# A recurrent layer on one core: its loop written out, its x blocks prefixed and transferred in halves, one product and three copies moved

## What is computed

```
x = x + attn0(rnn(x, cond))          # rnn: h = tanh(x_t @ Wx + h @ Wh + b), step by step, h kept for all t
x = x + ffn0(gru(x, cond))
x = x + attn1(logits(cond, x))       # gated linear attention
x = x + moe(lstm(x, cond))           # 8 experts, top 2
```

## Time and profile before

| | |
|---|---|
| time, median of 3 runs | 8,312.77 us (8,301.5 to 8,313.85) |
| time of the profiled execution | 8,311.89 us |
| its span | 8,310.0 us |
| mean granted TensorE clock | 0.951 |
| busy share: PE, DVE, ACT, POOL | 80%, 85%, 58%, 21% |
| recurrent layer | 0 to about 4,992 us |
| lead-in (9 x blocks) | about 44 to 280 us |

### The profile page before, as it was taken

How to read it: one execution, slowest core, us unless ns; L and a number is a source line. 1 busy time by engine, 2 the same in 40 slices (tenths; PEclk the granted TensorE clock), 3 DMA queues, 4 the chain that set the end, 5 groups by cost and what they waited for, 6 DMA issues and landing times. The chain is left out here.

```text
span 8310.0 us, 119850 instructions
## 1 busy us (share of the span) xinstructions
PE 6681.6 (80%) x37663; PEld 2690.1 (32%) x38193; DVE 7045.4 (85%) x12833; ACT 4836.8 (58%) x5718; POOL 1751.4 (21%) x1386
## 2 busy tenths in 40 slices
PE   4788888888888888888888882588888888782889
PEld 1233333333333333333333331122222222341553
DVE  4799999999999999999999996899999999446333
ACT  3677777777777777777777772233333333222322
POOL 0000001001001001001000010477777777000000
PEclk8999999999999999999999996899999999896999
DMA  1211111111111111111111110000000000000000
GB/s 37 37 27 32 32 27 32 32 27 32 30 29 32 27 32 32 27 32 32 27 32 31 28 32 24 19 3 3 4 3 3 4 3 3 2 6 3 3 15 5
DMA packets 51334, 174.57 MB, mean 21 GB/s; under 512 B 5857, under 2 KB 13794, under 8 KB 49698
## 3 DMA queue, kind: packets, MB, share of 16 engines
q0 software_dynamic: 37264, 145.91, 9.9%
q1 hardware_dynamic: 13586, 22.47, 1.0%
HBM read 15.12 MB, written 7.34 MB: 3 GB/s over the span
## 5 line engine op out<-in xcount | busy, mean ns | idle before, releaser
L964 POOL TENSOR_TENSOR hc<-hh,cg 128x512 f32<-128x512 f32 x1024 | 1296.1, 1268 | 510.4 <-DVE hh L947 510.4
L892 ACT ACTIVATE ps_m<-ps_m,aneg 128x508 f32<-128x508 f32 x1024 | 673.3, 658 | 1191.9 <-DVE hh L947 1069.6
L947 DVE TENSOR_TENSOR_SCAN hh<-ps_m,bx 128x512 f32<-128x512 f32 x1024 | 1228.0, 1204 | 0.0
L327 PE MATMUL r_ps<-wdiag,whq 128*128 128x512 bf16 x4224 | 998.2, 381 | 262.9 <-DVE rh_gain L190 106.6
L476 POOL TENSOR_TENSOR r_gate<-ident 128x1 f32<-128x1 f32 x137 | 213.7, 1560 | 4469.4 <-DVE rx_s L564 4404.4
L863 PE MATMUL ps_m<-hc,pick 128*128 128x512 f32 x2048 | 1054.1, 598 | 2.1 <-POOL hc L964 0.8
L571 DVE TENSOR_TENSOR_SCAN co<-rx_d 128x772 f32<-128x772 f32 x544 | 923.9, 1761 | 0.0
L571 DVE TENSOR_TENSOR_SCAN co<-rh_d 128x772 f32<-128x772 f32 x512 | 862.4, 1747 | 15.6
L300 PE MATMUL r_ps<-rx_nd,ident 128*128 128x512 f32 x1096 | 556.3, 654 | 195.5 <-DMA rx_nd<-rx_s 195.5
L929 DVE TENSOR_TENSOR bx<-ps_m,bg 128x512 f32<-128x512 f32 x1024 | 670.1, 659 | 49.2 <-PE ps_m L876 49.2
L327 PEld LDWEIGHTS r_ps<-wdiag,whq 128*128 128x128 bf16 x4480 | 396.1, 98 | 834.3 <-issue 134.2
(11 more groups left out here) (408 smaller groups left out, 11629.7 us busy)
## 6 DMA issues: line engine op xcount, KB each, us to landing
rx_nd<-rx_s POOLq DMA_DIRECT2D x137, 1040.0 KB, 8.0
rows_scratch<-pc SPq DMA_DIRECT2D x48, 128.0 KB
rows<-rows_scratch SPq DMA_DIRECT2D x128, 48.0 KB
ew<-in_e SPq DMA_DIRECT2D x3, 1024.0 KB, 7.1
co<-in_x_dn SPq DMA_DIRECT2D x1, 1024.0 KB, 4.7
xcur<-in_x_dn SPq DMA_DIRECT2D x1, 1024.0 KB
out_x<-xcur SPq DMA_DIRECT2D x1, 1024.0 KB, 3.9
qi<-in_f_q SPq DMA_DIRECT2D x1, 384.0 KB, 3.0
```

The costliest lines, as they stand in the source:

```text
L327: e.matmul(ps[:, bank, :], whq[:, 0, :], wdiag[:, 0, 0:N, :].rearrange("p m k -> p (m k)"), start=True, stop=True)
L892: e.activation(da[un % NDA][:, :, 1:T], ps[:, un % 2, :].rearrange("p (n t) -> p n t", n=NG4)[:, :, 1:T], ACT.Exp, scale=aneg[:, 0:1]).the ...
L947: e.tensor_tensor_scan(hh[un % NBUF][:], da[un % NDA].rearrange("p n t -> p (n t)"), bx[un % NBUF][:], 0.0, ALU.mult, ALU.add).then_inc(sc ...
L964: e.tensor_tensor(hc[un % NHC][:], hh[un % NBUF][:], cg[:], ALU.mult).then_inc(weighted, 1)
```

## The change

The hardware loop is replaced by all 128 steps written out, on every engine; thresholds become constants. The x even prefix is done in halves of the sequences, each behind its scan: the first half moves ahead of the h scans. The DMA that forms the x difference becomes two, each of 520 KB instead of one of 1,040 KB; the first is issued after the first half of the prefix. The operation on POOL ahead of it becomes a memset and is done for each half. On TensorE the x product of the next block moves from behind the x remainder to between its first pass (L295) and its second (L300); the wait for the h remainders' copies moves with it. On ScalarE `parts` is split: sums and differences stay where they are, the remainders' copies move behind the three tanh copies. The lead-in uses the halves as well, but its product stays where it was.

```diff
--- before.py
+++ after.py
-TURNS = 2
...
-            def remainder(bank0, F, stat, mov, prefixed, differenced, diff, last, own=NB, seeded=None):
+            def remainder(bank0, F, stat, mov, prefixed, differenced, diff, last, own=NB, seeded=None, between=None):
                 e.wait_ge(*prefixed)
                 for b in range(own):
                     e.matmul(ps[:, bank0 + b, :], negid[:], piece(F, "s", b), start=True, stop=False)
+                if between is not None:
+                    between()
                 e.wait_ge(*differenced)
...
-            with e.Fori(0, T // UN // TURNS) as turn:
-                for i, s in ((TURNS * turn + r, s) for r in range(TURNS) for s in range(UN)):
+            for i in range(T // UN):
+                for s in range(UN):
...
-                    remainder(0, X, xl_stat, x_mov((s + 1) % UN), (xs, 3 * g + 3), (xd, 16 * (g + 1)), x_diff, True).then_inc(xl_mm, 1)
-                    if s == UN - 2:
-                        e.wait_ge(stp, i + 3)
-                    e.wait_ge(ra, KA * t + A_PUT + 2 * NRC)
-                    product(4, xp_stat, x_mov((s + 2) % UN)).then_inc(xp_mm, 1)
+
+                    def next_product():
+                        if s == UN - 2:
+                            e.wait_ge(stp, i + 3)
+                        e.wait_ge(ra, KA * t + A_PUT + 2 * NRC)
+                        product(4, xp_stat, x_mov((s + 2) % UN)).then_inc(xp_mm, 1)
+
+                    remainder(0, X, xl_stat, x_mov((s + 1) % UN), (xs, 4 * g + 4), (xd, 32 * (g + 1)), x_diff, True,
+                              between=next_product).then_inc(xl_mm, 1)
                     e.wait_ge(xa, 5 * g + 5)
...
-            def parts(g, bank0):
-                e.wait_ge(xs, 3 * g + 3)
+            def put_known(g):
+                e.wait_ge(xs, 4 * g + 4)
                 put_sums(X, xa)
-                e.wait_ge(xd, 16 * (g + 1))
+                e.wait_ge(xd, 32 * (g + 1))
                 put_differences(X, X["nd"][:, :, 2:K2], xa)
+
+            def put_rest(g, bank0):
                 e.wait_ge(xl_mm, g + 1)
...
-                    parts(g, 0)
+                    put_known(g)
                     e.wait_ge(v, KV * t + V0 + VGUESS)
                     e.activation(t1[:, :, 2], gs[:, 1:NS + 1], ACT.Copy, scale=-1.0).then_inc(tri, 1)
                     e.activation(t1[:, :, 1], gs[:, 1:NS + 1], ACT.Copy).then_inc(tri, 1)
                     e.activation(t0[:, :, 0], line(xm), ACT.Copy).then_inc(tri, 1)
+                    put_rest(g, 0)
                     e.wait_ge(xa, 5 * g + 5)
...
             def x_difference(g):
                 e.wait_ge(xn, g + 1)
-                e.wait_ge(xs, 3 * g + 3)
-                e.wait_ge(xg, g + 1)
-                e.tensor_tensor(gate[:, 2:3], ident[:, 0:1], ident[:, 1:2], ALU.add).then_inc(xg, 1)
-                e.dma_start(flat(X["nd"][:]), flat(X["s"][:]), accum_op=ALU.add, max_dma_last_dim=4 * N * K2 // 2).then_inc(xd, 16)
+                for c, part in enumerate(HALVES):
+                    e.wait_ge(xs, 4 * g + 2 * (c + 1))
+                    e.wait_ge(xg, 2 * g + c + 1)
+                    e.memset(gate[:, 2:3], 0.0).then_inc(xg, 1)
+                    e.dma_start(flat(X["nd"][:, part]), flat(X["s"][:, part]), accum_op=ALU.add).then_inc(xd, 16)
...
-            def prefix_even(F):
-                return e.tensor_tensor(F["s"][:, :, 2:K2:2], F["s"][:, :, 1:D:2], F["pd"][:, :, 2:K2:2], ALU.add)
+            def prefix_even(F, part):
+                return e.tensor_tensor(F["s"][:, part, 2:K2:2], F["s"][:, part, 1:D:2], F["pd"][:, part, 2:K2:2], ALU.add)
...
-            def x_prefix_even(g):
-                e.wait_ge(xs, 3 * g + 2)
-                prefix_even(X).then_inc(xs, 1)
+            def x_prefix_even(g, c):
+                e.wait_ge(xs, 4 * g + 2 * c + 1)
+                prefix_even(X, HALVES[c]).then_inc(xs, 1)
...
                     x_prefix_odd(g, HALVES[0])
+                    x_prefix_even(g, 0)
...
                     x_prefix_odd(g, HALVES[1])
-                    x_prefix_even(g)
+                    x_prefix_even(g, 1)
                     x_chain(g - 1, s)
```

More of the change, by code:

```diff
@@ L343, in _ @@
                     e.wait_ge(stl, 2)
-                remainder(0, X, xl_stat, x_mov(g % UN), (xs, 3 * g + 3), (xd, 16 * (g + 1)), x_diff, True).then_inc(xl_mm, 1)
+                remainder(0, X, xl_stat, x_mov(g % UN), (xs, 4 * g + 4), (xd, 32 * (g + 1)), x_diff, True).then_inc(xl_mm, 1)
             e.wait_ge(xa, 5 * AHEAD + 1)
@@ L575, in x_prefix_odd @@
                 if later:
-                    e.wait_ge(xd, 16 * g)
+                    e.wait_ge(xd, 32 * g)
                 prefix_odd(X, part).then_inc(xs, 1)
-            def x_prefix_even(g):
-                e.wait_ge(xs, 3 * g + 2)
-                prefix_even(X).then_inc(xs, 1)
+            def x_prefix_even(g, c):
+                e.wait_ge(xs, 4 * g + 2 * c + 1)
+                prefix_even(X, HALVES[c]).then_inc(xs, 1)
             def x_chain(g, u):
@@ L591, in _ @@
             for g in range(AHEAD):
-                for part in HALVES:
-                    x_prefix_odd(g, part, g > 0)
-                x_prefix_even(g)
+                for c in range(2):
+                    x_prefix_odd(g, HALVES[c], g > 0)
+                    x_prefix_even(g, c)
                 if g:
@@ L607, in _ @@
                     tl.wait(j)
-                    j = tl.inc(prefix_even(R))
+                    j = tl.inc(prefix_even(R, slice(0, N)))
                     tl.wait(j)
```

## The result

The changed kernel takes 8,363.28 us (median, 8,359.55 to 8,366.68) where the kernel before takes 8,309.11 in the same comparison: ratio 1.0067, 95% interval 1.0055 to 1.008. It is slower, by 0.7%. The profiled execution took 8,359.55 us, its span is 8,357.7 us, and the forecast was 8,355.

A forecast was written before the change was run, and what follows sets the result against it. VectorE bounds undisturbed steps (35.89 us), a TensorE-ScalarE ring (35.69) takes over when x blocks are late. From 8,311.9 us, steps +77 (127 x (37.4 - 36.79)) and lead-in -34 give 8,355 us; range 8,325 to 8,400, chance 0.60.

The forecast's parts named there:

- The hole ahead of the fillers: TensorE's wait before the filler matmuls: 2.09 to 3.39 us, the clock falling onto the fillers in about nine of ten steps.
- The ring: Recurrent step through TensorE and ScalarE: 35.69 us, 35.84 after the change, plus 1.55 for the low clock: 37.4.
- Lead-in: Nine x blocks before the recurrent steps: 3.8 us less each, 34 us in all, bounds 20 and 38.
- Thresholds: Operations computing thresholds in the loop, replaced by constants: gain taken as 0, as the TensorE ring has hardly any.
- The copies' order: ScalarE's tanh copies ahead of the x remainders' copies: no loss, remainder copies start about 24.0 us after the recurrent prefix.
- The cover: On TensorE, the next x product stood between the last x pass and the fillers; moving its 1.30 us lengthens the hole.
- The early DMA: First half issued some 4 us after h: TensorE's wait of 1.00 us, 2.30 in late steps, goes and stays away.
- A: Rival, faster: the clock stays up and TensorE's ring is 35.84 us; 8,157 us, chance 0.14.
- B: Rival, faster: the fillers' queue doesn't bind either and VectorE's ring of 35.60 us holds; 8,127 us, chance 0.06.
- C: Rival: the clock falls in about half of the steps, +0.85 us, step 36.7; 8,267 us, chance 0.13.
- D: Rival, slower: the low clock outlasts 3.4 us and takes the h product too, step 38.4; 8,482 us, chance 0.06.
- E: Rival: the second DMA half lands 3 us later, holding L300 by 1 us, step 38.2; 8,455 us, chance 0.01.

The follow-up runs named there:

- x3: The changed kernel with only the copies of the x remainders back ahead of the tanh copies, product still between the passes: 8,361.63 us.
- y2: The kernel before with only the next x product moved between the two passes of the x remainder: 8,439.28 us.
- x1: The changed kernel with the next x product moved back behind the whole x remainder: 8,327.33 us.
- x2: The changed kernel with both the next x product and the copies of the x remainders back in their old places: 8,094.77 us.
- x4: The changed kernel with the first two groups of fillers left out, 20 of 28 left in each step: 8,152.04 us.
- y1: The kernel before with only its loop written out in 128 steps, single DMA kept: 8,190.35 us.
- z2: x2 with the loop of 16 written-out steps put back and the one-element addition as gate: 8,174.62 us.

## Why the prediction was right

*Sign and mechanism.* The hole ahead of the fillers, 3.39 predicted, is 3.06 by the row: 1.86 + 1.30 = 3.16 would have been the sum with the first filler counted. The fall came in 127 of 127 steps, where I had about nine of ten; it lies on the fillers; VectorE waits 2.0 us ahead of the recurrent prefix. x3 and y2 show that the product's move alone brings it, x1 that the copies' move alone does too, x2 that nothing else costs, x4 that most of the price is paid in the queue. The granted clock over the layer is 0.95; the 0.92 of the prediction doesn't fit its own low stretch of 3.4 us in a step of 37.4.

*The ring.* Predicted 35.84 + 1.55 = 37.4, measured 37.52. Both terms came out: the ring without the clock is 27.19 + 6.15 + 2.59 = 35.93, and the low clock costs 1.59, as the low stretch begins with the fillers and lies nearly whole on them. The 0.35 between ScalarE's copies and the fillers was mostly the missing record: by the first weight load it is 0.12 in the kernel before and 0.05 in the changed one, where the thresholds are constants.

*Lead-in.* Predicted -34, bounds 20 and 38; measured -45.1, outside them. The step that failed is the price of a block: 3.8 us, measured 25.4 to 26.8 down to 21.2, some 5. Gate and DMA gave less than I had: from the second gate to L301 it is 6.29 us (70.39 to 76.68) for 9.50 before, 3.2 less and not 4.1, as the second half lands 6.2 after its issue (I had 4.9). But the pass, which I had at nothing, takes 3.70 in every block where it took 5.16 to 6.62 (5.16 in the earlier trace rows, with a granted clock of 0.60 over 85.00 to 88.70). And ScalarE's copies, the floor that I named, now follow one another without idle time: the block of the earlier trace rows, 25.4, falls by 4.1 to that floor, and the longer ones fall to the same 21.2. That the total came within 5 us of the profiled execution is in part luck: the steps cost 17 us more than forecast, the lead-in gave 11 more. The estimate by the Trainium skill (DMA: Bandwidth & Descriptors, "Anatomy of one DMA"), 3.2 us for a half, is not what the trace shows: 4.6 us is the median of all halves.

*Thresholds.* Taken as 0; they cost VectorE 0.2 us a step. Undisturbed steps are 35.68 in y1 for 35.88 before, and 35.37 in x2 where I had 35.60. In the changed kernel that is hidden behind TensorE's ring.

*The copies' order.* I gave it no loss, and under the moved product it has none (x3). That rested on a tie, 24.0 against 24.0. Taken with the product in its old place the same order costs 233 us (x1 less x2). The cover was named and its loss not priced.

*The early DMA.* Wait of L300 gone, as forecast. That it is what ends the late steps was half right: they are gone with the single DMA too when the loop is written out (y1), and with the halves in a loop (z2).

*Rivals.* A (8,157) and B (8,127) name what happens without the fall: x2 ran at 8,095. C, D and E did not occur.

## What to carry to other kernels

Before a piece of work is moved off one place, price the hole that it leaves as well as the hole that it fills: here 1.3 us of matmuls bridged a wait, and with a hole of 3.06 us in place of 1.86 TensorE dropped to its lower clock once a step. Fillers that keep a clock up stand in the same queue as real work; when the clock falls they are what delays it. Several edits made together can hide a gain of 2.5% behind a loss: undo them one by one and in pairs, since here neither of the two alone brought it back. And count the records of a row before a time is read from it: one missing matmul shifted a hole by 0.23 us here.

## What was not expected

- The step settled at one length, 37.42 to 37.57 us in 110 of 127 steps (some 37.8 in 16), with the low stretch at the same place in all but the first: 33.0 to 33.2 us after h. In x4_19_fillers it came in every other step over long stretches. The fall doesn't come at random in these.
- Writing the loop out was worth 114 us of 8,305 (y1), of which the turns are 41: constants in place of computed thresholds gave about 25 more by the length of undisturbed steps, and the end of late steps the rest.
- Two half DMAs issued 1.4 us apart in the lead-in landed 5.9 to 6.2 us after the second issue (70.43 to 76.68 in the block shown), where the median of all is 4.6; the whole one took 8.0.
